# Spacing a maximum pass, starting kept blocks one unit earlier, and moving a normalisation ahead of exponentials

## What is computed

```python
q = einsum('qc,bcn->bqn', Wq, xf); k = einsum('qc,bcn->bqn', Wk, xf); v = einsum('vc,bcn->bvn', Wv, xf)
attn = softmax(einsum('bqn,bqm->bnm', q, k) * scale, axis=-1)
out = einsum('bvm,bnm->bvn', v, attn)
x = gamma[0] * einsum('oc,bchw->bohw', Wo, out) + x
```

```python
low = prelu(bn(einsum('oc,nchw->nohw', mag_w, low) + mag_b))
hs  = concatenate([high, roll(high, 1, axis=2)], axis=1)
hs  = prelu(bn(einsum('oc,nchw->nohw', phase_w, hs) + phase_b))
out = up2_nearest(low) + hs[:, :C]
```

## Time and profile before

| | |
|---|---|
| median of 3 runs | 2341.36 us (2339.72 to 2341.66) |
| profiled execution | 2340.45 us, span 2338.5 us |
| TensorE busy | 2205.9 us, 94% |
| VectorE busy | 1782.4 us, 76% |
| ScalarE busy | 1431.6 us, 61% |
| GpSimd busy | 677.7 us, 29% |
| granted TensorE clock, mean | 0.984 of full speed |
| 16 DMA engines, mean | 101 GB/s |

### The profile page before, as it was taken

How to read it: one execution, slowest core, us unless ns; L and a number is a source line. 1 busy time by engine, 2 the same in 40 slices (tenths; PEclk the granted TensorE clock), 3 DMA queues, 4 the chain that set the end, 5 groups by cost and what they waited for, 6 DMA issues and landing times.

```text
span 2338.5 us, 48099 instructions
## 1 busy us (share of the span) xinstructions
PE 2205.9 (94%) x16373; PEld 1764.1 (75%) x16373; DVE 1782.4 (76%) x3388; ACT 1431.6 (61%) x2547; POOL 677.7 (29%) x891
## 2 busy tenths in 40 slices
PE   5799999999989999999998999999999999999997
PEld 4577777777767777777777777777777777777776
DVE  6777877777867788877786877777877777778764
ACT  3457666657656666666656666566665656666663
POOL 3232332232322323322232321323322232233321
PEclk8799999999999999999999999999999999999998
DMA  4254444454554444444474443443445444344443
GB/s 159 59 115 94 99 109 102 84 117 99 135 131 85 110 107 92 109 108 97 93 168 102 99 99 72 104 96 91 103 111 133 75 89 93 77 82 88 84 86 64
DMA packets 596617, 235.02 MB, mean 101 GB/s; under 512 B 547072, under 2 KB 548352, under 8 KB 596576
## 3 DMA queue, kind: packets, MB, share of 16 engines
q1 hardware_dynamic: 596576, 234.51, 45.5%
HBM read 67.67 MB, written 32.53 MB: 43 GB/s over the span
## 4 chain that ended last, share of the span: by engine, by line
PE 64%; DVE 15%; issue 10%; DMA 5%; ACT 3%; POOL 1%; SPq 1%; DVEq 0%; ACTq 0%; POOLq 0%
PE M L482 13%; PE M L519 7%; PE O L631 7%; PE O L633 6%; PE O L632 6%; PE O L644 6%; PE O L646 6%; PE O L645 6%; DVE pq L1052 5%; DMA pt<-pq 4%; PE S L590 4%; DVE saved L947 4%; DVE pmax L943 2%; DVE pl L1047 2%; PE M L500 1%
## 5 line engine op out<-in xcount | busy, mean ns | idle before, releaser
L758 ACT ACTIVATE ph<-S 128x512 f16<-128x512 f32 x512 | 307.6, 601 | 525.5 <-PE S L590 524.8
L644 PE MATMUL O<-uh,pt 128*128 128x257 f16 x2048 | 568.2, 277 | 16.9 <-DMA pt<-pq 16.7
L631 PE MATMUL O<-uh,ph 128*128 128x257 f16 x2048 | 570.3, 278 | 4.5 <-DVE pl L1047 4.1
L633 PE MATMUL O<-uh,pl 128*128 128x257 f16 x2048 | 563.2, 275 | 0.0
L632 PE MATMUL O<-ul,ph 128*128 128x256 f16 x2048 | 561.8, 274 | 0.0
L646 PE MATMUL O<-uh,pt 128*128 128x257 f16 x2048 | 559.0, 273 | 0.0
L645 PE MATMUL O<-ul,pt 128*128 128x256 f16 x2048 | 555.7, 271 | 0.0
L947 DVE TENSOR_SCALAR_CACHE_REDUCE saved<-M 128x512 f32<-128x512 f32 x512 | 344.0, 687 | 257.0 <-PE M L519 253.0
L1047 DVE TENSOR_TENSOR pl<-p,ph 128x512 f16<-128x512 f32 x512 | 402.6, 787 | 60.5 <-ACT p L761 59.1
L519 PE MATMUL M<-kst,qst 96*128 (+1 forms) x1024 | 424.0, 442 | 20.9 <-DVE saved L947 16.2
L1052 DVE TENSOR_TENSOR pq<-saved,pq 128x512 f16<-128x512 f32 x512 | 387.6, 757 | 19.2 <-ACT saved L770 19.1
(11 more groups left out here) (161 smaller groups left out, 2907.4 us busy)
## 6 DMA issues: line engine op xcount, KB each, us to landing
xr<-in_x SPq DMA_DIRECT2D x53, 512.0 KB, 3.8
out_y<-z SPq DMA_DIRECT2D x33, 512.0 KB, 3.0
xb<-in_x SPq DMA_DIRECT2D x25, 512.0 KB, 3.7
pt<-pq SPq DMA_TRANSPOSE x512, 3.1
qraw<-q_scratch SPq DMA_DIRECT2D x99, 64.0 KB, 2.0
uh_scratch<-uh_next SPq DMA_DIRECT2D x24, 257.0 KB, 3.2
uh<-uh_scratch SPq DMA_DIRECT2D x24, 257.0 KB, 3.2
ul_scratch<-ul_next SPq DMA_DIRECT2D x24, 256.0 KB, 3.1
```

The source lines that it names most:

```text
L631: nc.tensor.matmul(O[j][:, 0:UW], ph[:, i % 4, q], uh[:, i, :], start=(i == 0), stop=False)
L633: ins = nc.tensor.matmul(O[j][:, 0:UW], pl[:, i % 4, q], uh[:, i, :], start=False, stop=False)
L644: nc.tensor.matmul(O[j][:, 0:UW], pt[:, k % RING, i, :], uh[:, t, :], start=False, stop=False)
```

## The change

`DOUBLE` changes from steps 11, 13, 15, 16, 18, 25 to 9, 13, 17, 22, 24, 26. The kept blocks' exponentials move one step earlier (from 5 to 6 steps ahead of their weighing), and their low parts to 4 steps ahead, which is one step earlier for blocks 0 to 9 and no change for 10 to 15. `SCAN` moves from step 20 to 22 and `QUERIES` from 27 to 28, so behind the last maximum, which stays in step 28. On SP the transposing DMA of kept block 2 is issued ahead of the output's store instead of behind it. On ScalarE the tasks `low` of a step are taken ahead of its kept exponentials; the others stay behind them.

With the banks beside them, the tasks of a FULL turn from step 20 are, before: low 0 (M1), max (M0) | low 1 (M1), max (M0) | high 0 (M1), max (M0) | max (M1) | high 1 (M0), max (M1) | max (M0), max (M1) | and one maximum a step up to 28. After: low 0 (M1), max (M0) | low 1 (M1), max (M0) | high 0 (M1), max (M0), max (M1) | max (M0) | high 1 (M1), max (M0), max (M1) | max (M0) | max (M1), max (M0) | max | max. At the head of a turn ScalarE's list is, before: in step 0 kq, u 0, probabilities 2; 1: probabilities 3, kept 0; 2: probabilities 4, u 1; 3: probabilities 5, kept 1. After: 0: kept 0, kq, u 0, probabilities 2; 1: probabilities 3; 2: probabilities 4, kept 1, u 1; 3: probabilities 5.

```diff
-ROUND_X, ROUND_CONV, SCAN, NEGATIVE, QUERIES = 9, 14, 20, 26, 27
-
-DOUBLE = (11, 13, 15, 16, 18, 25)
+ROUND_X, ROUND_CONV, SCAN, NEGATIVE, QUERIES = 9, 14, 22, 26, 28
+
+DOUBLE = (9, 13, 17, 22, 24, 26)
...
-EXP_AT = [AT["k", k] - 5 for k in range(NK)]
-LOW_AT = [AT["k", k] - (3 if k < ND - RISE else 4) for k in range(NK)]
+EXP_AT = [AT["k", k] - 6 for k in range(NK)]
+LOW_AT = [AT["k", k] - 4 for k in range(NK)]
...
+                turn_slot(g, 2)
                 sp.wait_ge(out_ready, g + 1)
                 gp = (g + (ALL - 2)) % ALL
                 sp.dma_start(out_v[ds(gp // NCH, 1), ds(gp % NCH, 1)], z[:, :, :]).then_inc(out_stored, 16)
-                turn_slot(g, 2)
...
+                    for n, task in plan.numbered.get(t, []):
+                        if task[0] == "low":
+                            act.wait_ge(m_filled[n % 2], use(plan, g, n) + 1)
+                            norm_low(M[n % 2], g, task[1:], m_free[n % 2])
                     for k in range(NK):
                         if EXP_AT[k] == t:
                             slot_probabilities(g, k)
                     for n, task in plan.numbered.get(t, []):
                         bank = M[n % 2]
-                        if task[0] in ("kq", "u", "low", "high"):
+                        if task[0] in ("kq", "u", "high"):
                             act.wait_ge(m_filled[n % 2], use(plan, g, n) + 1)
-                        if task[0] == "low":
-                            norm_low(bank, g, task[1:], m_free[n % 2])
-                        elif task[0] == "high":
+                        if task[0] == "high":
                             norm_high(bank, g, task[1], m_free[n % 2])
-                        else:
+                        elif task[0] != "low":
                             take(bank, task, g, parity, c)
```

## The result

The changed kernel takes 2351.87 us (median, 2350.91 to 2353.58) against 2341.36 (2339.72 to 2342.63): a ratio of 1.0047, 95% interval 1.0032 to 1.0061. It is slower by 10.5 us; forecast were 2357 and slower. The changed kernel's profiled execution has a span of 2348.8 us.

The account below looks back on a forecast made before the run. TensorE's queue and its waits were taken to bound the kernel (busy 68.0 of 70 us a turn). Costs of 87.8 less gains of 72.0 made +15.8 us, 2357 from the median 2341.36; the range was 2337 to 2374.

Parts of the forecast that it names:

- the 1.5 for the cast: The moved cast stands before the queries' last step, which had 0.9 to spare: 0.05 a turn, 1.5 us cost.
- Pairs of maxima behind the convolutions: Steps 22 and 24: second maximum waits for ScalarE's normalisation of its bank; costs 41.5 in FULL, 6.9 in LAST turns.
- The head: Turn start: earlier exponentials delay ScalarE; 1.37 lost in each of 21 FULL turns, 29.4 with 0.6 more; LAST turns 8.5.
- Low normalisation: Taken ahead of the kept exponentials, it ends the high convolution's wait: 24 x 0.74 = 17.8 us gained.
- The negated maxima: Their transposes wait for the last maximum behind the cast; moving the cast wins 24 x 0.57 = 13.7 us.
- The wait for block 2: TensorE's DMA wait at kept block 2 goes whole: 13.5 + 27 x 0.26 = 20.5 us gained.
- The maxima: Spacing ends the waits for VectorE around steps 15 to 17, 16.4 us, and step 13's longer weighing gap, 3.6.
- The last row of steps: Step 24: block 14's pair just passes after block 10's transpose; priced at 0, up to 0.6 if that takes 3.7.
- The rule on the shared port: VectorE's last low part contends with GpSimd and grows by up to 0.3; some 7 us more, outside the sum.

Follow-up runs that it names:

- both edits: Changed kernel with double steps 9, 13, 17, 23, 25, 26 and kept blocks 0 and 1 put back to their old steps: 2259.33 us, 0.9657 of the kernel before.
- the lead: Kernel before with kept blocks 2 to 15 given one unit more of lead (exponentials 6 steps ahead, low parts 4), nothing else: 2315.64 us, 0.9894.
- the spacing alone: Kernel before with double steps 9, 13, 17, 23, 25, 26 and nothing else: 2332.57 us, 0.9968.

## Why the prediction was right, and where it wasn't

The sign and the mechanism were right: two new stalls a turn and one at the head outweigh what the reordering takes away. The costs that both edits take away were 92.5 us where I had 86.3 (87.8 with the 1.5 for the cast), gains 81.7 where I had 72.0.

- *Pairs of maxima behind the convolutions*, 48.4 forecast, 60.6 measured. The stall at step 22 is 0.87 (1.11 less the usual 0.24) where 0.88 was forecast. Two terms were too small: a weighing behind a maximum that has waited starts 0.35 after it and not 0.24, and in LAST turns I counted only 0.1 for the second pair, since VectorE's tail held TensorE there anyway. But VectorE's tail starts with that maximum: behind it VectorE is never idle for more than 0.27 until the negated maxima. So what delays it delays the tail: the full 1.95.
- *The head*, 37.9 forecast, 32.6 measured. The stall is 1.36 against my 1.37 and shows in 21 FULL turns; about 0.14 of it comes back within the turn. In LAST turns the wait at weighing 3 isn't longer (0.23); instead the first maximum waits 0.66 for the split queries (qst L941), which stand behind the same late pl 2. Same sum, other place.
- *Low normalisation*, 17.8 forecast, 17.7 alone.
- *The negated maxima*, 13.7 less 1.5 forecast, 18.3 alone. I gave the LAST turns nothing, and they win 0.9 each (their wait is 0.96 in the changed kernel, where I expected over 1), while FULL turns win 0.5 and not 0.57; the 1.5 I took off for the queries behind the cast don't exist: no scores wait for qcur in an ordinary turn.
- *The wait for block 2*, 20.5 forecast. The order on SP alone gives 9.5; without it the lead leaves the wait whole. The cause named was right, but a part of the gain is lost again where VectorE isn't on time for the next maxima, and I had counted the whole of it.
- *The maxima*, 16.4 + 3.6 forecast for the spacing. This step failed as I put it: either edit removes the listed waits, but with the spacing alone the time is lost again between its maxima and the weighings, and only the lead wins it. The spacing is worth 6.7 us alone, 3.5 beside the lead and 2.9, not told from nothing, at the end. The sum survived because both edits are in the change, and that is luck: the lead's 24.1 us had no term of its own.
- *The last row of steps*: the waiting pair of block 14 was priced at 0 and costs up to 0.1.
- *The rule on the shared port*: the last low part takes 0.83 behind the negative parts, where it took 0.83 in the kernel before; it did not grow, and the 7 us beside the sum did not come.

That net 10.5 lies so near to 15.8 is partly luck: the LAST turns lost 6 to 8 us more by the second pair and won 6 more by the cast.

## What to carry to other kernels

Where tasks take two buffers in turn, look at who empties the buffer two tasks back, not at how evenly the tasks lie: the same number of maxima cost 60 us when two of them followed a task whose bank another engine empties, and nothing a step later. Moving work earlier in an in-order queue pays only where that queue is ahead; at the head of the turn ScalarE was the late one, and a unit of lead for two blocks cost 33 us there while it gave 24 on the other fourteen. When one reordering has several parts, run each of them alone: here the edit aimed at a wait (the spacing) took the wait away and hardly any time, and another (the lead) took the time.

## What the runs showed of the hardware

The cast of the queries took 0.94 us in 31 of 32 turns of the kernel before and takes 0.41 in all 32 now (0.42 in the first), though GpSimd is adding up z beside it both times. VectorE's rows at the end of a FULL turn, and GpSimd's:

```profile
513.05 0.69 DVE L949 TENSOR_SCALAR_CACHE_REDUCE saved<-M 128x512 f32<-128x512 f32 x1
...
514.01 0.21 DVE L956 TENSOR_SCALAR nmax<-nmax 128x4 f32<-128x4 f32 x1
514.25 0.65 DVE L958 TENSOR_SCALAR nbias<-nmax 128x4 f32<-128x4 f32 x1
514.82 0.41 DVE L962 CAST qcur<-qst 96x512 fp32r<-96x512 f32 x1
...
512.34 3.48 POOL L1220 TENSOR_TENSOR z<-z,zneg 128x256 f32<-128x256 f32 x4
```

The small operation on the maxima (L956) fell from 0.43 to 0.21 as well. The move of the cast alone does it: in that run the cast takes 0.41 and the small operation 0.21 too, and with the spacing alone they stay at 0.94 and 0.43. The Trainium skill, "SBUF — State Buffer", section "Who interferes with whom", lets casts and `tensor_scalar` operations take the port pair that VectorE shares with GpSimd, whoever issues first holding it; 0.94 against 0.41 fits a cast that first waits for one of GpSimd's additions. That it was this wait wasn't tested by itself, and nothing in the rows says why the new place is free of it.
